# Two layers of a recommendation tower, turned from one tile of samples with samples on the partitions to two tiles with features on the partitions

## The chip, the cores and the metric

The kernel runs on one core of one Trainium2 chip. The metric is device time in microseconds. Short names: PE is TensorE, ACT ScalarE, DVE VectorE, POOL GpSimd, SP SyncE.

## What is computed

512 samples, each with 26 indices into 26 embedding tables of width 128 and one dense vector of width 128. Everything is f32.

```python
e = jnp.stack([tbl_0[ids[:, 0]], ..., tbl_25[ids[:, 25]]], axis=1)
combined = jnp.concatenate([dense_features[:, None, :], sparse_features], axis=1)
interactions = jnp.einsum('bfd,bgd->bfg', combined, combined)
z = interactions[:, iu, ju]                      # 351 pairs
h = jnp.concatenate([z, r_dense_features], axis=1)
h = jnp.maximum(h @ W_top1 + b_top1, 0.0)        # 479 -> 512
h = jnp.maximum(h @ W_top2 + b_top2, 0.0)        # 512 -> 256
y = h @ W_top3                                   # 256 -> 1
```

## The kernel before, in words

The samples form four tiles of 128 (`T = 4`). A factor of a product that must keep f32 accuracy is split in a rounded part "hi" and a rest "lo" (both f32r), and three products are taken: hi·hi, hi·lo, lo·hi. ACT makes the hi (a copy that rounds), DVE the lo (a subtraction).

**Selection.** For the 12 smallest tables (1000 rows) the lookup is a product of the table with one-hot rows: six steps of two tables, each 8 chunks of 125 rows, both parts, 512 samples as columns (`select_first`, `select_step`). The ids are spread over the partitions by a product (`spread_ids`) or by a DMA; DVE makes 7 of the 8 one-hot chunks of a step (`make_onehots`), ACT the eighth (`make_last_onehot`). Step 0 is written out in `select_first`: eight products of table 0's hi as the chunks come, with the ids of step 1 spread between the fourth and the fifth, then 24 more. `stage` holds 4 tables, `tab_hi` and `tab_lo` 4.

**Gathered rows.** The other 14 tables are gathered by POOL, 128 rows per indirect DMA, 14 per tile, 56 in all, in the order of the tiles into two row buffers. PE transposes them in groups of 4, 4, 4, 2 (`transpose_group(t, q)`), ACT and DVE copy the result to `feats` (`copy_turn`).

**Pairs.** `gram(t, h)` makes the pair products of a quarter of a tile, 32 products of 27 columns, in one of `GB = 3` PSUM banks; it waits for the pick three quarters back (`picked_by_dve`). ACT and DVE pick from it (`copy_picked`); DVE reorders a tile (`order_by_sample`), PE transposes it (`move_picked`), ACT and DVE split it (`split_hi`, `split_lo`).

**Layers.** Per tile: layer 1 is 15 products of 512 columns (3 for the dense vector, 12 for the pairs), samples on the output's partitions. Relu on ACT (`relu1`), four transposes on PE (`transpose_hidden`), the split, layer 2 as 12 products of 256 columns plus one that adds the bias (L465), and layer 3 as a multiply and row sum on DVE (`finish`). The last tile does layer 1 in two halves of 256 columns (L498 to L505). At the end y, a column per tile, is transposed on PE (L575), copied (L921) and stored.

Each engine works in the order in which its block is written. `turns` lists the users of the PSUM banks for transposes in their order. All waits are on semaphores; a later instruction of an engine never passes an earlier one.

## Time and profile before

| | |
|---|---|
| median of 3 runs | 113.29 us (112.92 to 114.68) |
| profiled execution | 114.23 us; its span 112.4 us |
| PE busy | 102.7 us (91%), weight loads beside it 79.6 us |
| DVE, ACT, POOL busy | 66.8, 56.9, 61.0 us |
| selection on PE ends | 58.2 us into the span |
| last gather of rows issued | 79.05 us |
| DMA moved | 13.12 MB, 117 GB/s over the span |

The span runs from the first to the last instruction of the profiled execution; 1.8 us of its time lie around it. The busy share of PE says that it nearly always has something in flight, not that it goes at its best pace: a product of 512 columns takes one duration at the higher clock and nearly twice that at the lower.

### The profile page before, as it was taken

To read this page: it belongs to the slowest core of one execution; us is meant where nothing else is said; L and a number is where in the kernel's file an instruction comes from. 1 tells how busy PE (TensorE), PEld (TensorE's weight loads), DVE (VectorE), ACT (ScalarE), POOL (GpSimd) and SP (SyncE) were. 2 spreads that over 40 slices of the span, in tenths; PEclk is the share of its full clock that TensorE was granted. 3 is DMA by queue.
4 is the path that set the end of the run, shared out by engine and by line. 5 is a ranking of instruction groups with operands and counts; after the bars stand their busy time and mean duration, and the time that the engine had idled before them with its cause. 6 is when DMAs were issued, how large, how long until landed. Compare 5 with 4: busy or idle time off the path is not lost.

```text
span 112.4 us, 3333 instructions
## 1 busy us (share of the span) xinstructions
PE 102.7 (91%) x1447; PEld 79.6 (71%) x1447; DVE 66.8 (59%) x113; ACT 56.9 (51%) x83; POOL 61.0 (54%) x63
## 2 busy tenths in 40 slices
PE   4679999999999999999999839999999999988981
PEld 4235777788888888888887627786868786668860
DVE  1499846999999998996001976326331652252132
ACT  2596900894984956998028427047014701152210
POOL 2787877777777777778777767777300000000000
PEclk9999999999999999999999985999999999999997
DMA  2999789999999995482121212222100000000000
GB/s 60 289 272 228 204 148 274 235 258 223 250 172 244 246 346 198 121 271 62 47 67 50 53 47 53 53 71 51 47 6 6 0 6 0 6 6 0 0 0 1
DMA packets 5885, 13.12 MB, mean 117 GB/s; under 512 B 1784, under 2 KB 2698, under 8 KB 5871
## 3 DMA queue, kind: packets, MB, share of 16 engines
q1 hardware_dynamic: 3018, 8.37, 27.1%
q0 software_dynamic: 1792, 3.67, 12.7%
q10 hardware_dynamic: 1060, 0.87, 5.4%
q8 instruction: 11, 0.18, 0.7%
q14 instruction: 4, 0.02, 0.1%
HBM read 12.89 MB, written 0.01 MB: 115 GB/s over the span
## 4 chain that ended last, share of the span: by engine, by line
PE 90%; DVE 4%; ACT 2%; issue 2%; POOL 0%; DVEq 0%; POOLq 0%
PE banks L369 33%; PE banks L407 11%; PE banks L352 6%; PE banks L389 6%; PE banks L344 4%; PE banks L438 4%; PE banks L444 3%; PE banks L439 3%; PE banks L329 3%; PE banks L470 3%; PE banks L415 2%; PE banks L317 2%; PE banks L471 2%; PE banks L477 1%; DVE ids_bc L825 1%
## 5 line engine op out<-in xcount | busy, mean ns | idle before, releaser
L308 POOL DMA_INDIRECT rows<-in_tbl,ids_sb x56 | 60.3, 1076 | 18.2 <-issue 16.1
L369 PE MATMUL banks<-onehots,tab_hi 125*128 125x512 f32 x80 | 31.6, 395 | 0.0
L369 PE MATMUL banks<-onehots,tab_lo 125*128 125x512 f32 x80 | 31.2, 390 | 0.0
L611 ACT ACTIVATE tab_hi<-stage 125x1024 fp32r<-125x1024 f32 (+1 forms) x12 | 11.9, 1016 | 11.6 <-PE banks L369 5.8
L369 PEld LDWEIGHTS banks<-onehots,tab_hi 125*128 125x128 f32 x80 | 15.0, 188 | 3.3 <-issue 0.4
L369 PEld LDWEIGHTS banks<-onehots,tab_lo 125*128 125x128 f32 x80 | 15.0, 188 | 3.0
L798 DVE TENSOR_SCALAR onehots<-ids_bc,row_of 125x1024 fp32r<-125x1024 f32 x21 | 14.3, 750 | 2.5 <-PE banks L352 2.4
L407 PEld LDWEIGHTS banks<-feats 128*27 128x27 f32 x1024 | 10.9, 106 | 6.3 <-DVE picked L815 3.3
L785 DVE TENSOR_TENSOR tab_lo<-stage,tab_hi 125x1024 fp32r<-125x1024 f32 x12 | 14.2, 1219 | 1.0 <-ACT tab_hi L611 1.0
L815 DVE COPY_PREDICATED picked<-second_of,banks 128x112 f32<-128x112 int32 x16 | 4.5, 281 | 16.8 <-ACT picked L668 16.8
L798 DVE TENSOR_SCALAR onehots<-ids_bc_h,row_of 125x1024 fp32r<-125x1024 int16 x21 | 14.4, 752 | 0.0
L407 PE MATMUL banks<-feats 128*27 128x27 f32 x1024 | 13.1, 194 | 0.8 <-issue 0.5
L668 ACT ACTIVATE picked<-banks 128x112 f32<-128x112 f32 x16 | 4.2, 263 | 18.5 <-PE banks L407 18.3
L644 ACT ACTIVATE feats<-banks 128x1024 f32<-128x1024 f32 x6 | 6.7, 1115 | 5.1 <-PE banks L369 5.1
L389 PE MATMUL banks<-ident,rows 128*128 128x128 f32 x56 | 8.6, 278 | 0.1
L779 DVE TENSOR_TENSOR onehots<-stage,onehots 128x1024 fp32r<-128x1024 f32 (+1 forms) x3 | 3.1, 1029 | 9.0 <-ACT onehots L605 9.0
L389 PEld LDWEIGHTS banks<-ident,rows 128*128 128x128 f32 x56 | 6.3, 141 | 1.8 <-issue 1.0
L661 ACT ACTIVATE feats<-banks 128x512 f32<-128x512 f32 (+1 forms) x10 | 6.5, 693 | 0.6 <-PE banks L389 0.6
L636 ACT ACTIVATE onehots<-distance 125x1024 fp32r<-125x1024 f32 x6 | 6.3, 1050 | 0.2 <-PE banks L369 0.2
L344 PE MATMUL banks<-onehots,tab_hi 125*128 125x512 f32 x8 | 4.8, 728 | 1.8 <-DVE onehots L798 1.8
L842 DVE TENSOR_TENSOR tab_lo<-banks,tab_hi 128x512 fp32r<-128x512 f32 (+1 forms) x5 | 2.9, 578 | 5.7 <-ACT tab_hi L653 5.7
L438 PE MATMUL banks<-onehots,pairs_hi 128*128 128x512 f32 x12 | 5.9, 491 | 0.0
(81 smaller groups left out, 131.6 us busy)
## 6 DMA issues: line engine op xcount, KB each, us to landing
stage<-in_tbl SPq DMA_DIRECT2D x11, 448.0 KB
stage<-in_w SPq DMA_DIRECT2D x3, 512.0 KB
rows<-in_tbl,ids_sb POOLq DMA_INDIRECT x56, 6.0
ids_bc_h<-ids_short_rows ACTq DMA_DIRECT2D x6, 128.0 KB, 6.6
stage<-in_tbl SPq DMA_DIRECT2D x11, 52.0 KB
stage<-in_tbl SPq DMA_DIRECT2D x2, 224.0 KB
dense_sb<-in_dense SPq DMA_DIRECT2D x1, 256.0 KB, 11.7
stage<-in_w SPq DMA_DIRECT2D x1, 256.0 KB
```

Source lines behind the costliest of these rows:

```text
L308: nc.gpsimd.indirect_dma_start(out=rows[:, t % RB, m, :], out_offset=None, in_=tables[m], in_offset=bass.IndirectOffsetOnAxis(ap=ids_sb[:, ...
L344: nc.tensor.matmul(bank(0, 0), tab_part(0, 0)[:, c, :], onehots[0:RP, c, 0, :], start=(c == 0), stop=False)
L352: last = nc.tensor.matmul(bank(0, k), tab_part(k, part)[:, c, :], onehots[0:RP, c, k, :], start=(part == 0 and c == 0), stop=(part == 1 an ...
L369: last = nc.tensor.matmul(bank(n, k), tab_part(i, part)[:, c, :], onehots[0:RP, c, k, :], start=(c == 0 and part == 0), stop=(c == CHUNKS ...
L389: last = nc.tensor.transpose(tr_ps(n)[:, c, :], rows[:, t % RB, m, :], ident[:])
L407: last = nc.tensor.matmul(gram_ps(u)[SLOT * s:SLOT * s + F, i, 0:F], x, x, start=True, stop=True)
L438: nc.tensor.matmul(l1_ps, x, w1_hi[:, k, :], start=False, stop=False)
L611: nc.scalar.activation(tab_part(i, 0)[:, first:, :], src[:, first:, :], ACT.Copy).then_inc(hi_ready, 1)
L644: nc.scalar.activation(dst, src, ACT.Copy).then_inc(selected_copied, 1)
L661: nc.scalar.activation(dst, src, ACT.Copy).then_inc(turn_by_act, 1)
L785: nc.vector.tensor_tensor(tab_part(i, 1), src, tab_part(i, 0).bitcast(f32), ALU.subtract).then_inc(lo_ready, 1)
L798: nc.vector.tensor_scalar(onehot(n, c), ids_of(n)[0:RP], row_of[:, c:c + 1], None, ALU.is_equal).then_inc(onehot_by_dve, 1)
```

## The change

Layers 1 and 2 now run for two tiles at once (`PT = 2`), with the features on the output's partitions: the weights are the stationary operand, and 256 samples are the columns. Layer 1 of a pair is four blocks `m` of 128 features, each 15 products of 256 columns; relu and split go straight from PSUM to the layer 2 operand, without the transposes. Layer 2 is 4 pieces of 6 products (two output blocks `m`), its bias is added by ACT and DVE with the relu (`relu2`), and layer 3 is two f32 products with a stationary operand of one column; y comes out as a row and is stored in two DMAs. `b_top2` and `W_top3` are loaded as four rows and turned once on PE (`turn_small`). The layers of tiles 0 and 1 start when both are split. Layer 2 of that pair stands ahead of the transposes of tile 3's last group. In the selection, WARM goes from 8 to 6 transposes of the identity, another six stand behind the first `spread_ids`, and two (`FILL`) behind each of the first seven products.

```diff
-    C1 = H1 // P
-    HH, CH = H1 // 2, C1 // 2
+    C1, C2 = H1 // P, H2 // P
+    PT = 2
+    PN = PT * P
+    NP = T // PT
...
-    WARM = 8
+    WARM = 6
+    FILL = 2
...
+    turns = [(t, q) for t in (0, 1) for q in range(NG)] + [moved(0), (2, 0), (2, 1), moved(1)]
+    turns += [(2, 2), (2, 3), (3, 0), (3, 1), moved(2), (3, 2), (3, 3), moved(3)]
...
+        def l1_ps(n):
+            return banks[:, 6 + n % 2, 0:PN]
+        def l2_ps(m):
+            return banks[:, 1 + m, 0:PN]
+        def y_ps(p):
+            return banks[0:1, 0, PN * p:PN * (p + 1)]
...
+                    if c < CHUNKS - 1:
+                        warm_up(FILL)
...
+            def turn_small():
+                pe.wait_ge(small_loaded, 32)
+                pe.wait_ge(ids_copied, BY_DMA)
+                nc.tensor.transpose(banks[:, 7, 0:2 * C2], b2w3_rows[:], ident[0:2 * C2, 0:2 * C2]).then_inc(
+                    rows_turned, 1)
...
+            def layer1_dense(p, m):
+                n = C1 * p + m
+                if n == 0:
                     pe.wait_ge(ids_copied, BY_DMA)
                     pe.wait_ge(dense_lo_ready, 1)
                     pe.wait_ge(lo_ready, S + 1)
+                elif n == 1:
+                    pe.wait_ge(b2w3_ready, 1)
...
+            def layer1(p, m):
+                n = C1 * p + m
+                cols = slice(P * m, P * (m + 1))
+                pe.wait_ge(pairs_hi_ready, PT * (p + 1))
+                for k in range(1, NK + 1):
+                    if n == 0:
                         pe.wait_ge(lo_ready, S + k // WS + 1)
+                    x = pairs_hi[:, k - 1, :, :]
+                    nc.tensor.matmul(l1_ps(n), w1_hi[:, k, cols], x, start=False, stop=False)
+                    nc.tensor.matmul(l1_ps(n), w1_lo[:, k, cols], x, start=False, stop=False)
+                pe.wait_ge(turn_by_dve, dve_turns(turns.index(moved(PT * p + 1)) + 1))
                 for k in range(1, NK + 1):
+                    last = nc.tensor.matmul(l1_ps(n), w1_hi[:, k, cols], pairs_lo[:, k - 1, :, :], start=False,
                                             stop=(k == NK))
                 last.then_inc(layer1_done, 1)
+            def layer2(p, c):
+                if c == 0 and p == 0:
                     pe.wait_ge(lo_ready, S + WV + 1)
+                if c == 0:
+                    pe.wait_ge(picked_by_dve, U * (T - 1) if p == 0 else U * T - 1)
+                pe.wait_ge(h1T_hi_ready, C1 * p + c + 1)
+                hi, lo = h1T_hi[p][:, c, :], h1T_lo[p][:, c, :]
+                for m in range(C2):
+                    cols = slice(P * m, P * (m + 1))
+                    nc.tensor.matmul(l2_ps(m), w2_hi[:, c, cols], hi, start=(c == 0), stop=False)
+                    nc.tensor.matmul(l2_ps(m), w2_lo[:, c, cols], hi, start=False, stop=False)
+                pe.wait_ge(h1T_lo_ready, C1 * p + c + 1)
+                for m in range(C2):
+                    cols = slice(P * m, P * (m + 1))
+                    last = nc.tensor.matmul(l2_ps(m), w2_hi[:, c, cols], lo, start=False, stop=(c == C1 - 1))
+                    if c == C1 - 1:
+                        last.then_inc(layer2_done, 1)
+            def layer3(p):
+                if p == 0:
+                    pe.wait_ge(picked_by_dve, U * T)
                 else:
+                    pe.wait_ge(y_ready, p)
+                for c in range(C2):
+                    pe.wait_ge(h2T_by_act if c == 0 else h2T_by_dve, p + 1)
+                    last = nc.tensor.matmul(y_ps(p), b2w3[:, C2 + c:C2 + c + 1], h2T[p][:, c, :], start=(c == 0),
+                                            stop=(c == C2 - 1))
+                last.then_inc(layer3_done, 1)
...
             spread_ids(0)
+            warm_up(WARM)
...
             gram(0, 2)
-            layer1_dense(0)
             gram(0, 3)
+            gram(1, 0)
             move_picked(0)
...
+            gram(1, 1)
+            gram(1, 2)
+            gram(1, 3)
+            transpose_group(2, 0)
+            transpose_group(2, 1)
+            turn_small()
+            layer1_dense(0, 0)
+            move_picked(1)
+            transpose_group(2, 2)
+            transpose_group(2, 3)
+            layer1(0, 0)
+            layer1_dense(0, 1)
+            layer1(0, 1)
+            gram(2, 0)
+            layer1_dense(0, 2)
+            layer1(0, 2)
+            gram(2, 1)
+            gram(2, 2)
+            gram(2, 3)
+            transpose_group(3, 0)
+            transpose_group(3, 1)
+            layer1_dense(0, 3)
+            layer1(0, 3)
+            move_picked(2)
+            transpose_group(3, 2)
+            for c in range(C1):
+                layer2(0, c)
+            transpose_group(3, 3)
+            for h in range(U):
+                gram(3, h)
+            layer1_dense(1, 0)
+            layer1_dense(1, 1)
+            move_picked(3)
+            layer1(1, 0)
+            layer3(0)
+            layer1(1, 1)
+            layer2(1, 0)
+            layer1_dense(1, 2)
+            layer1(1, 2)
+            layer2(1, 1)
+            layer1_dense(1, 3)
+            layer1(1, 3)
+            layer2(1, 2)
+            layer2(1, 3)
+            layer3(1)
...
+            def hidden_hi(p, m):
+                n = C1 * p + m
+                act.wait_ge(layer1_done, n + 1)
+                nc.scalar.activation(h1T_hi[p][:, m, :], l1_ps(n), ACT.Relu).then_inc(h1T_hi_ready, 1)
+            def relu2(p):
+                act.wait_ge(layer2_done, C2 * p + 1)
+                nc.scalar.activation(h2T[p][:, 0, :], l2_ps(0), ACT.Relu, bias=b2w3[:, 0:1]).then_inc(h2T_by_act, 1)
...
             make_hi(S + 2)
+            copy_picked(1, 0)
             split_hi(0)
             for v in range(3, WV + 1):
                 make_hi(S + v)
...
+            copy_picked(1, 1)
+            copy_picked(1, 2)
+            copy_picked(1, 3)
+            copy_turn(2, 0)
+            copy_turn(2, 1)
+            copy_small()
+            split_hi(1)
+            hidden_hi(0, 0)
+            hidden_hi(0, 1)
+            copy_picked(2, 0)
+            hidden_hi(0, 2)
+            copy_picked(2, 1)
+            copy_picked(2, 2)
+            copy_picked(2, 3)
+            copy_turn(3, 0)
+            copy_turn(3, 1)
+            hidden_hi(0, 3)
+            split_hi(2)
+            relu2(0)
+            for h in range(U):
+                copy_picked(3, h)
+            split_hi(3)
+            for m in range(C1):
+                hidden_hi(1, m)
+            relu2(1)
...
+            def hidden_lo(p, m):
+                n = C1 * p + m
+                dve.wait_ge(h1T_hi_ready, n + 1)
+                nc.vector.scalar_tensor_tensor(h1T_lo[p][:, m, :], l1_ps(n), 0.0, h1T_hi[p][:, m, :].bitcast(f32),
+                                               ALU.max, ALU.subtract).then_inc(h1T_lo_ready, 1)
+            def relu2(p):
+                if p == 0:
+                    dve.wait_ge(b2w3_ready, 1)
+                dve.wait_ge(layer2_done, C2 * p + 2)
+                nc.vector.tensor_scalar(h2T[p][:, 1, :], l2_ps(1), b2w3[:, 1:2], 0.0, ALU.add, ALU.max).then_inc(
+                    h2T_by_dve, 1)
...
             split_lo(0)
             for v in range(3, WV + 1):
                 make_lo(S + v)
...
+            for h in range(U):
+                copy_picked(1, h)
+            order_by_sample(1)
+            split_lo(1)
+            copy_turn(2, 2)
+            copy_turn(2, 3)
+            hidden_lo(0, 0)
+            hidden_lo(0, 1)
+            copy_picked(2, 0)
+            hidden_lo(0, 2)
+            copy_picked(2, 1)
+            copy_picked(2, 2)
+            copy_picked(2, 3)
+            order_by_sample(2)
+            hidden_lo(0, 3)
+            split_lo(2)
+            copy_turn(3, 2)
+            relu2(0)
+            copy_turn(3, 3)
+            for h in range(U):
+                copy_picked(3, h)
+            order_by_sample(3)
+            split_lo(3)
+            hidden_lo(1, 0)
+            copy_y(0)
+            for m in range(1, C1):
+                hidden_lo(1, m)
+            relu2(1)
+            copy_y(1)
```

Three places show how the instructions now stand. **The start on PE**, before the second step of the selection; `ident` is the identity (the transposes of `warm_up`), `pairs_hi` holds the ids here. Before:

```order
L317 MATMUL banks<-ident 128x128 x8
L329 MATMUL banks<-pairs_hi,ident_r 128x512 x2
L344 MATMUL banks<-onehots,tab_hi 128x512 x4
L329 MATMUL banks<-pairs_hi,ident_r 128x512 x2
L344 MATMUL banks<-onehots,tab_hi 128x512 x4
L352 MATMUL banks<-onehots,tab_hi 128x512 x8
L352 MATMUL banks<-onehots,tab_lo 128x512 x16
L329 MATMUL banks<-pairs_hi,ident_r 128x512 x2
```

And with the change, up to the id-spread for step 1:

```order
L318 MATMUL banks<-ident 128x128 x6
L330 MATMUL banks<-pairs_hi,ident_r 128x512 x2
L318 MATMUL banks<-ident 128x128 x6
L345 MATMUL banks<-onehots,tab_hi 128x512
L318 MATMUL banks<-ident 128x128 x2
L345 MATMUL banks<-onehots,tab_hi 128x512
L318 MATMUL banks<-ident 128x128 x2
L345 MATMUL banks<-onehots,tab_hi 128x512
L318 MATMUL banks<-ident 128x128 x2
L345 MATMUL banks<-onehots,tab_hi 128x512
L318 MATMUL banks<-ident 128x128 x2
L330 MATMUL banks<-pairs_hi,ident_r 128x512 x2
```

The products of chunks 0 to 6 now have two transposes of the identity behind each, and six more stand between the first id-spread and the first product.

**DVE after tile 0's pairs** (`stage3`, `w2` and `w` hold the second layer's weights, `picked1` the pairs of tile 1). Before:

```order
L825 STREAM_TRANSPOSE ids_bc0<-picked0 128x512
L779 TENSOR_TENSOR onehots<-stage2,onehots 128x512
L832 TENSOR_TENSOR pairs_lo0<-banks,pairs_hi0 128x512
L772 TENSOR_TENSOR w2_lo<-stage3,w2_hi 128x1024
L898 SCALAR_TENSOR_TENSOR b2_rows<-b2_hi,minus_lower,b2_sb 2x256
L815 COPY_PREDICATED picked1<-second_of,banks 128x14x8 x4
```

And with the change:

```order
L805 STREAM_TRANSPOSE ids_bc0<-picked0 128x512
L759 TENSOR_TENSOR onehots<-stage2,onehots 128x512
L812 TENSOR_TENSOR pairs_lo<-banks,pairs_hi 128x4x128
L752 TENSOR_TENSOR w2_lo<-stage3,w2_hi 128x1024
L795 COPY_PREDICATED picked1<-second_of,banks 128x14x8 x4
L805 STREAM_TRANSPOSE ids_bc1<-picked1 128x512
```

The order is the same but for the bias row (L898), which is gone; what moves is PE's order beside it.

**PE between tile 0's last transposes of rows and tile 1's pairs** (`feats` are pair products, 32 to a quarter, each of them two instructions in the trace; the transposes with `ids_bc` are `move_picked`). Before:

```order
L419 MATMUL banks<-onehots,dense_hi 128x512
L420 MATMUL banks<-onehots,dense_hi 128x512
L421 MATMUL banks<-onehots,dense_lo 128x512
L407 MATMUL banks<-feats 27x27 x32
L415 MATMUL banks<-ident,ids_bc 128x128 x4
L407 MATMUL banks<-feats 27x27 x32
L438 MATMUL banks<-onehots,pairs_hi 128x512
L439 MATMUL banks<-onehots,pairs_hi 128x512
L438 MATMUL banks<-onehots,pairs_hi 128x512
L439 MATMUL banks<-onehots,pairs_hi 128x512
L407 MATMUL banks<-feats 27x27 x32
```

And with the change:

```order
L414 MATMUL banks<-feats 27x27 x96
L422 MATMUL banks<-ident,ids_bc 128x128 x4
L414 MATMUL banks<-feats 27x27 x96
L392 MATMUL banks<-ident,rows 128x128 x8
L429 MATMUL banks<-ident,b2w_rows 128x4
L445 MATMUL banks<-dense_hi,onehots 128x256
L446 MATMUL banks<-dense_lo,onehots 128x256
L447 MATMUL banks<-dense_hi,onehots 128x256
L422 MATMUL banks<-ident,ids_bc 128x128 x4
```

Layer 1's products of tile 0 stood between the quarters of tile 1; now a quarter of tile 1 stands ahead of `move_picked(0)` and the other three follow it back to back, ahead of every product of layer 1.

## Rows read from the trace of the kernel before

**Rows 1.** the page: the chain that ended last, by engine.
```profile
PE 90%; DVE 4%; ACT 2%; issue 2%; POOL 0%; DVEq 0%; POOLq 0%
```

**Rows 2.** timeline to 22 us: start, length, engine, line, count, idle before.
```profile
1.52 1.97 PE L317 MATMUL banks<-ident 128*128 128x128 f32 x8 [1.52 <-POOL ident L299]
...
2.54 0.42 DVE L861 CAST pairs_hi<-feats 12x512 fp32r<-12x512 int32 x1 [0.66 <-DMA feats<-in_ids_rows]
...
3.42 1.22 PE L329 MATMUL banks<-pairs_hi,ident_r 12*128 12x512 f32 x2
...
5.51 4.74 DVE L798 TENSOR_SCALAR onehots<-ids_bc,row_of 125x1024 fp32r<-125x1024 f32 x7
...
6.41 2.69 PE L344 MATMUL banks<-onehots,tab_hi 125*128 125x512 f32 x4 [1.77 <-DVE onehots L798]
...
12.05 3.61 PE L352 MATMUL banks<-onehots,tab_hi 125*128 125x512 f32 x8
...
15.46 3.90 PE L352 MATMUL banks<-onehots,tab_lo 125*128 125x512 f32 x16
...
19.94 0.50 PE L369 MATMUL banks<-onehots,tab_hi 125*128 125x512 f32 x1
...
21.05 1.06 ACT L611 ACTIVATE tab_hi<-stage 125x1024 fp32r<-125x1024 f32 x1 [0.54 <-DMA stage<-in_tbl]
```

**Rows 3.** ACT's timeline, the second step's share (same columns).
```profile
23.87 1.12 ACT L644 ACTIVATE feats<-banks 128x1024 f32<-128x1024 f32 x1
```

**Rows 4.** chain of waits, in the selection: start, length, what.
```profile
27.51 0.44 PE banks L389 x4
...
58.21 1.06 ACT feats L644
```

**Rows 5.** windows of PE: us, busy (instructions), granted clock, DMA share, GB/s.
```profile
67.00:68.00 1.00, 1.00 (x43) 0.50 0.22 57
...
70.00:71.00 1.00, 1.00 (x57) 0.87 0.28 66
```

**Rows 6.** PE's timeline round the pause after tile 0.
```profile
66.64 0.96 PE L415 MATMUL banks<-ident,ids_bc 128*128 128x128 f32 x4 [1.80 <-DVE ids_bc L825]
```

**Rows 7.** DVE's timeline in the same place.
```profile
69.21 1.23 DVE L772 TENSOR_TENSOR w_lo<-stage,w_hi 128x1024 fp32r<-128x1024 f32 x1 [0.25 <-ACT w_hi L599]
...
70.75 0.27 DVE L815 COPY_PREDICATED picked<-second_of,banks 128x112 f32<-128x112 int32 x1
```

**Rows 8.** ACT's timeline in the same place.
```profile
68.13 1.05 ACT L599 ACTIVATE w_hi<-stage 128x1024 fp32r<-128x1024 f32 x1
```

**Rows 9.** PE's timeline: a tile at full clock, the last tile, the end.
```profile
85.99 0.74 PE L407 MATMUL banks<-feats 128*27 128x27 f32 x64
86.66 1.09 PE L389 MATMUL banks<-ident,rows 128*128 128x128 f32 x8
...
90.33 0.38 PE L465 MATMUL banks<-b_rows,ones 2*128 2x256 f32 x1
90.65 0.39 PE L470 MATMUL banks<-w_hi,tab_hi 128*128 128x256 f32 x1
...
101.61 0.39 PE L498 MATMUL banks<-onehots,pairs_hi 128*128 128x256 f32 x1 [0.69 <-ACT pairs_hi L674]
101.83 0.28 PE L499 MATMUL banks<-onehots,pairs_hi 128*128 128x256 f32 x1
101.95 0.28 PE L498 MATMUL banks<-onehots,pairs_hi 128*128 128x256 f32 x1
...
110.00 0.38 PE L575 MATMUL banks<-ident,y 128*4 128x128 f32 x2 [0.59 <-DVE stage L852]
```

**Rows 10.** weight loads by line: count, busy, mean ns, idle before.
```profile
L498 PEld LDWEIGHTS banks<-onehots,pairs_hi 128*128 128x128 f32 x8 | 1.5, 188 | 0.9 <-ACT pairs_hi L674 0.9
```

**Rows 11.** DVE's last row, same columns.
```profile
110.42 0.37 DVE L921 COPY stage<-banks 4x128 f32<-4x128 f32 x1 [0.47 <-PE banks L575]
```

**Rows 12.** POOL's last gather of rows.
```profile
79.05 0.94 POOL L308 DMA_INDIRECT rows<-in_tbl,ids_sb  x1 [0.30 <-issue]
```

## What the change should do to the time

> **What bounds the kernel now.** I read the page's chain of waits first: 90% of it lies on PE and 4% on DVE [rows 1]. So it is PE's own work and pauses that count, and the other engines only where PE waits for them. Then the timeline of the first 22 us, to see which clock PE works at; the chain in the selection; PE, DVE and ACT round PE's one long pause; and PE in an undisturbed tile and at the end. Three things are to be seen.
>
> First, the start runs at PE's lower clock. Eight products of 512 columns lie between 12.05 and 15.46, 0.43 us each, which is 1.2 GHz; from 15.46 sixteen take 3.90, 0.235 each, which is 2.4 GHz [rows 2]. The second step's first product starts at 19.94. Before about 10 us the products stand 0.66 apart ([rows 2]: four in 2.69) because DVE makes a one-hot every 0.68 (seven in 4.74).
>
> Second, the selection then runs without a gap to 58.2, and the rest to the end of DVE's last instruction, 110.42 + 0.37 = 110.79, takes 52.6 [rows 4, 11].
>
> Third, within this rest PE pauses 1.80 us before 66.64 [rows 6]; the clock is at 0.50 (1.2 GHz) at 67 and is back at 2.4 GHz within the slice at 70 [rows 5]. An undisturbed quarter of pair products takes 86.66 - 85.99 = 0.67, a product of 256 columns 0.115, a transpose 0.44/4 = 0.11, and where PE turns to another kind of work the first step is 0.1 longer (101.61 to 101.83 against 101.95) [rows 4, 9].
>
> **The sum, against the profiled execution (114.23 us).**
>
> *1. Id-spread earlier: -0.4.* The ids are ready at 2.54 + 0.42 = 2.96, but the spread waits for eight transposes until 3.42 [rows 2]. With six it starts at about 3.0, and DVE's one-hots at 5.1.
>
> *2. Transposes between the first products: -1.3 with step 1 in it.* The six further transposes (about 0.21 each at the lower clock) fill PE's wait. A chunk with its two is 0.43 + 2 x 0.21 = 0.85 at the lower clock, 0.46 at the higher; DVE delivers every 0.68. So PE has no gap from about 6.0, where it now has none only from the second id-spread on. The question is when the clock rises. Before, it rose at about 15.5, some 5 us after the gaps ended; after the pause it rose about 4 us after 66.64 [rows 2, 5, 6]. From 6.0 that gives 10 to 11, perhaps 7 if the work ahead of 5.4 counts. With a rise at 11, chunk 4 is under way; three more chunks take 0.46 each and 24 products 0.235 each, and with the id-spread (0.65) the second step starts near 18.6, 1.3 earlier; with a rise at 7 it starts near 16.9, 3.1 earlier; with none before 15.5 at 20.7, 0.75 later, since the added transposes then cost and give nothing. I take a gain of 1.7, near the later rise, which has the better row.
>
> There is a cap. ACT's rounding of table 5 waits for its DMA until 21.05, and three ACT instructions later the copy of step 0 ends at 23.87 + 1.12 = 24.99 [rows 2, 3], which step 2 waits for. With four transposes (0.44) step 2 can start at 25.4 instead of 27.95 [rows 4]. So at most 2.5 of the 3.1 survive. DVE needs 7 x 0.68 + 2 x 1.2 = 7.2 a step against PE's 7.7, so the gain is kept to the end of the selection. Terms 1 and 2: **-1.7**, ends -2.5 and +0.75.
>
> *3. The tail, in the times of the trace (its start left at 58.2).* Up to tile 0's third quarter nothing changes. The fourth quarter and tile 1's first then go before the pause, which stays for the same cause (DVE's reorder of tile 0, before 66.64 [rows 6]); I put `move_picked(0)` at 66.25. Two quarters follow, until 68.15. Then tile 1's fourth quarter needs DVE's pick of its first (three banks). On DVE that pick stands behind the split of `w2`, which starts at 69.21 and takes 1.23, behind ACT's rounding (68.13 + 1.05) [rows 7, 8]. Before, the pick ran at 70.75 and hurt nobody, since layer 1's products stood between. Now PE waits from 68.15 to about 69.95: a **new pause of 1.8 us**. The quarter ends at 70.65, where before it ended at about 75.0 with tile 0's 12 layer products done.
>
> From there, all at the higher clock: 40 transposes x 0.115 = 4.6; layer 1, 8 blocks x 15 x 0.115 = 13.8; layer 2, 48 x 0.117 = 5.6; layer 3, two f32 products of 256 columns twice. The f32 product of 128 columns at 110.00 takes 0.38 with its pipeline's end, 0.21 without [rows 9], so 4 x 0.43 = 1.7; ends 1.5 and 2.2. Eight quarters x 0.67 = 5.4; about 20 changes of kind x 0.1 = 2.0. Pauses: the copy of tile 3's last group on DVE before its pairs 0.6; reorder before `move_picked(3)` 0.7; the split after it 0.7 (the row at 101.61 has that same wait [rows 9]); relu before layer 3 0.6. Then the copy of y, 0.5. Sum 36.2, end at 106.9, against 110.79: -3.9.
>
> What this tail leaves out is in there: sixteen hidden transposes (1.8), four bias products (90.33 to 90.65, 0.32 each, 1.3 [rows 9]) and the y transposes with their wait (1.0), less layer 3 (1.7).
>
> *4. The clock in the tail: +1.4.* The old pause cost one stretch at 1.2 GHz, and that is in 110.79. The new one comes 1.9 us later and should keep the clock down until 73 or 74. The work there is a quarter (0.94 instead of 0.67), eight transposes (+0.8) and a few layer products (+0.3). Ends: nothing, and 2.6 if two stretches fall outside the pauses. Terms 3 and 4: **-2.5**, ends -3.9 and -1.0.
>
> *What costs nothing.* The layer 2 block that stands ahead of tile 3's last transposes only keeps PE off POOL: the last gather is issued at 79.05 [rows 12], PE comes there near 88, so neither order waits. The turn of the small rows is one short transpose. Relu and split of 256 columns on ACT and DVE lie beside the next block's 15 products (1.7 us), and layer 1 alternates two banks. The first half of y is stored beside PE's work.
>
> Sum: 114.23 - 1.7 - 2.5 = 110.0. The profiled execution lies 0.94 above the median, so the median should be **109.1 us**.
>
> **A rule against this change.** The last tile already has layer 1 products of 256 columns: sixteen weight loads of 0.188 each [rows 10] lie in stretches where the products are 0.115 apart [rows 9], so loads overlap and splitting 512 into twice 256 is free. The Trainium skill (TensorE: Matmul & The Clock Gate, section Back-to-back issue gap) says that load and product set the spacing together, about 81 ns at 128 columns and 131 at 512. By that rule two of 256 cost well above one of 512, and an estimate from those figures makes layer 1 dearer by about half, the sum by 7 us. The trace's 0.115 is half of its 0.235, which speaks against it.
>
> **Rivals.**
> - *The clock does not rise earlier in the selection.* Terms 1 and 2 become 0 to +0.75. For: until 10 us PE worked with short gaps before too, and the clock did not rise. Time: 109.1 + 2.0 = 111.1. Chance 0.15.
> - *The tail gives back what it saves.* DVE's order makes tile 1 pay longer, the clock stays low twice, and waits for relu and split between layers add up. Tail -0.5, time 111.1. Chance 0.18. Both of these together: 113.2, chance 0.06.
> - *Both go better:* clock up near 7, none lost in the tail: 109.1 - 0.8 - 1.4 = 106.9. Chance 0.05.
> - *Slower: weight loads become the bound of the layers.* If a load could not start before its predecessor ended, each of the 120 layer 1 products would take 0.188 instead of 0.115 [rows 9, 10]: +8.7, time 117.8. It decides from a spacing of 0.115 + 4.2/120 = 0.15 on. For: the stationary operand is now a strided slice of `w1`, which no row shows, and every load is a new one. Against: the last tile. The rule above is a milder form of it. Chance 0.03.
> - The forecast itself, 107.9 to 110.4: chance 0.53.
>
> **How the numbers follow.** A measurement of this kernel tells 2% (2.3 us) from no change. Faster means under 111.0: the forecast, the better case, half of each of the two rivals at 111.1 and none of the rest: 0.53 + 0.05 + 0.16 = 0.74. Slower: the loads, and a part of what I have not seen: 0.04. Same: 0.22. The range from 107.4 to 112.2 leaves out the better case's lower part, the double miss and the loads.
>
> **What would show it.** Right: the 24 products of the first step start near 12.4 instead of 11.6 but at 0.235 each; the second step before 18.8; the selection ends near 56.5; a second PE pause of over 1.5 us before tile 1's fourth quarter, released by DVE's pick, with `w2`'s split ahead of it; clock 0.50 for more than one stretch round it; layer products 0.115 to 0.12 apart; no wait for gathered rows in tile 3; from the selection's end to DVE's last copy about 50.1. Wrong: products of 256 columns over 0.15 apart, a clock that rises only at 15, or layer blocks that wait for relu and split.

## The result, and the profile after

The changed kernel is **slower**: 116.94 us median of five runs (116.6 to 120.5) against 114.13 us of the kernel before in the same runs; the ratio is 1.031, 95% interval 1.022 to 1.040. (Executions of either kernel fall in a shorter and a longer group; the ratio compares the means of the shorter ones, 116.9 and 113.4, here and in every ratio below.) Forecast were 109.1 us and a range up to 112.2. The profiled execution took 119.35 us, span 117.5, so it lies 2.4 above the median; the executions at 116.6 to 116.9 have spans of 114.7 to 115.0. A later profile of the same kernel, below, has a start that is 2.6 us shorter.

The page: PE's row, the granted clock in 40 slices, the instruction queue, the chain by engine (it answers [rows 1]).

```profile
PE 104.1 (89%) x1497; PEld 86.4 (74%) x1497; DVE 67.4 (57%) x109; ACT 55.8 (47%) x82; POOL 61.9 (53%) x63
...
PEclk9999999999999999999999687559999999599999
...
q8 instruction: 12, 0.20, 0.7%
...
PE 81%; issue 7%; ACT 5%; DVE 4%; POOL 0%; DVEq 0%; POOLq 0%
```

"issue" is 7% of the chain, 8 us, where it was 2%. The clock is low in three stretches of the tail (in windows: 65 to 69, 72 to 79 and 99 to 103 us), where it was in one. PE works 1.4 us longer in all, so most of the loss is standing still. PE's timeline at the start (columns: start, length, engine, line, count, idle before it), for [rows 2]:

```profile
3.00 1.21 PE L330 MATMUL banks<-pairs_hi,ident_r 12*128 12x512 f32 x2
...
8.42 0.63 PE L318 MATMUL banks<-ident 128*128 128x128 f32 x2
...
14.12 1.99 PE L355 MATMUL banks<-onehots,tab_hi 125*128 125x512 f32 x8
15.95 3.79 PE L355 MATMUL banks<-onehots,tab_lo 125*128 125x512 f32 x16
19.67 0.72 PE L330 MATMUL banks<-pairs_hi,ident_r 12*128 12x512 f32 x2
```

The first id-spread is at 3.00, as forecast, but a product with its two transposes stays at 0.85 us until 14.12, and the second step starts at 20.32, 0.4 later than before, not 1.7 earlier. The row at 19.67 is the third id-spread, the last work ahead of the second step. The column of the granted clock reads 1.00 in windows from 7 to 17 us all the same, so I read the clock of the start from the spacing: 512 columns take 0.43 at the lower clock and 0.23 at the higher. Then PE's tail, from the last product of the selection to the end:

```profile
58.20 0.39 PE L372 MATMUL banks<-onehots,tab_lo 125*128 125x512 f32 x1
...
62.24 1.46 PE L414 MATMUL banks<-feats 128*27 128x27 f32 x90
65.00 1.71 PE L414 MATMUL banks<-feats 128*27 128x27 f32 x102 [1.30 <-issue]
67.26 1.12 PE L422 MATMUL banks<-ident,ids_bc 128*128 128x128 f32 x4 [0.55 <-DVE ids_bc L805]
68.31 2.06 PE L414 MATMUL banks<-feats 128*27 128x27 f32 x128
71.46 0.35 PE L414 MATMUL banks<-feats 128*27 128x27 f32 x21 [1.09 <-DVE picked L795]
72.50 0.76 PE L414 MATMUL banks<-feats 128*27 128x27 f32 x43 [0.69 <-issue]
73.19 1.97 PE L392 MATMUL banks<-ident,rows 128*128 128x128 f32 x8
...
75.67 0.41 PE L446 MATMUL banks<-dense_lo,onehots 128*128 128x256 f32 x1
75.88 0.41 PE L447 MATMUL banks<-dense_hi,onehots 128*128 128x256 f32 x1
```

```profile
85.54 1.15 PE L414 MATMUL banks<-feats 128*27 128x27 f32 x112 [0.21 <-issue]
...
89.46 0.28 PE L457 MATMUL banks<-pairs_hi,onehots 128*128 128x256 f32 x1 [0.91 <-issue]
...
95.21 2.06 PE L414 MATMUL banks<-feats 128*27 128x27 f32 x211 [0.81 <-issue]
99.28 0.70 PE L414 MATMUL banks<-feats 128*27 128x27 f32 x45 [2.02 <-issue]
...
103.27 0.39 PE L457 MATMUL banks<-pairs_hi,onehots 128*128 128x256 f32 x1 [0.69 <-ACT pairs_hi L665]
...
114.38 1.02 PE L491 MATMUL banks<-distance,b2w 128*1 128x256 f32 x4 [0.54 <-ACT distance L644]
```

A quarter of pair products is x64. The new pause that I forecast before tile 1's fourth quarter is there, released by DVE's pick, with 1.09 us. But there are five more that nothing releases: 1.30 after 90 rows of L414, 0.69 after 21, 0.21 after 80, 0.91 in the middle of a layer 1 block, and 2.02 after 211 rows that had no pause among them. Together 5.13 us. None is at the edge of a quarter, where PE's program has its waits. (The 0.81 before 95.21 is called "issue" too, but stands at such an edge, where PE waits for DVE's copy of tile 3's last group; I had forecast 0.6 for it.) Layer products of 256 columns are 0.12 apart at the higher clock, and there is no wait for gathered rows. DVE's last instruction:

```profile
115.44 0.59 DVE L830 COPY y_row<-banks 1x256 f32<-1x256 f32 x1 [1.08 <-PE banks L491]
```

It ends at 116.03. From the selection's end at 58.6 that is 57.4 us; before it was 52.6 ([rows 4, 11]), and forecast was 50.1.

### The profile page after: what moved, and what is told of

It is laid out like the page before. It is cut to its first block, busy times and chain, and to the rows that moved or that the text cites. A ratio compares the mean times of both kernels' runs of the same rounds, so it can differ in the third digit from the quotient of the medians.

```text
span 117.5 us, 3417 instructions
## 1 busy us (share of the span) xinstructions
PE 104.1 (89%) x1497; PEld 86.4 (74%) x1497; DVE 67.4 (57%) x109; ACT 55.8 (47%) x82; POOL 61.9 (53%) x63
## 4 chain that ended last, share of the span: by engine, by line
PE 81%; issue 7%; ACT 5%; DVE 4%; POOL 0%; DVEq 0%; POOLq 0%
PE banks L372 31%; PE banks L414 7%; PE banks L392 5%; PE banks L355 5%; PE banks L457 4%; PE banks L318 4%; PE banks L345 3%; PE banks L458 3%; PE banks L461 3%; PE banks L422 3%; PE banks L330 3%; PE banks L445 2%; PE banks L491 2%; PE banks L475 2%; PE banks L476 2%
## 5 line engine op out<-in xcount | busy, mean ns | idle before, releaser
L309 POOL DMA_INDIRECT rows<-in_tbl,ids_sb x56 | 61.1, 1090 | 18.1 <-issue 16.2
L372 PE MATMUL banks<-onehots,tab_hi 125*128 125x512 f32 x80 | 31.7, 396 | 0.0
L414 PE MATMUL banks<-feats 128*27 128x27 f32 x1024 | 13.3, 198 | 6.6 <-issue 5.0
L414 PEld LDWEIGHTS banks<-feats 128*27 128x27 f32 x1024 | 11.4, 110 | 9.1 <-issue 6.5
L818 DVE SCALAR_TENSOR_TENSOR tab_lo<-banks,tab_hi 128x256 fp32r<-128x256 f32 x8 | 3.4, 425 | 14.0 <-ACT tab_hi L640 14.0
L640 ACT ACTIVATE tab_hi<-banks 128x256 fp32r<-128x256 f32 x8 | 3.1, 384 | 15.5 <-PE banks L461 15.5
L457 PE MATMUL banks<-pairs_hi,onehots 128*128 128x256 f32 x32 | 8.6, 299 | 1.6 <-issue 0.9
L392 PE MATMUL banks<-ident,rows 128*128 128x128 f32 x56 | 9.8, 313 | 0.0
L318 PE MATMUL banks<-ident 128*128 128x128 f32 x26 | 7.5, 424 | 1.5 <-POOL ident L300 1.5
L392 PEld LDWEIGHTS banks<-ident,rows 128*128 128x128 f32 x56 | 7.8, 162 | 0.8
L458 PE MATMUL banks<-pairs_hi,onehots 128*128 128x256 f32 x32 | 8.1, 284 | 0.0
```

The costliest lines, as they stand in the source:

```text
L309: nc.gpsimd.indirect_dma_start(out=rows[:, t % RB, m, :], out_offset=None, in_=tables[m], in_offset=bass.IndirectOffsetOnAxis(ap=ids_sb[:, ...
L318: nc.tensor.transpose(banks[:, 4, 0:P], ident[:], ident[:])
L372: last = nc.tensor.matmul(bank(n, k), tab_part(i, part)[:, c, :], onehots[0:RP, c, k, :], start=(c == 0 and part == 0), stop=(c == CHUNKS ...
L392: last = nc.tensor.transpose(tr_ps(n)[:, c, :], rows[:, t % RB, m, :], ident[:])
L414: last = nc.tensor.matmul(gram_ps(u)[SLOT * s:SLOT * s + F, i, 0:F], x, x, start=True, stop=True)
L457: nc.tensor.matmul(l1_ps(n), w1_hi[:, k, cols], x, start=False, stop=False)
```

## Theories

**Theory A: delivery of instructions.** A row of PE is a weight load and a product, so two instructions; a quarter is 128 in 0.67 us, a layer block of 15 products 30 in 1.75. The instruction queue (q8) moved 12 packets, 0.20 MB, that is 16 KB each; I take one for a block of 256 instructions. If one block is fetched while the one before it runs, and takes longer than two quarters, PE stands still wherever the 256th instruction falls. From row 90 of 62.24 to row 21 of 71.46 there are 102 + 4 + 128 + 21 = 255 rows, 510 instructions: two blocks but for two, and the program's own waits, which are instructions too, stand in no row. The kernel before has a quarter between each two blocks of layer 1; the changed one has four in a row, twice. **Rivals:** the pauses are waits for banks, picks or copies; the clock; the new start; layers of two tiles cost more by themselves.

The Trainium skill (Runtime: NRT & Kernel Launch, section Instruction fetch mechanics) describes refills of 16 KiB, 256 instructions, and calls the cost of crossing a block "mostly hidden". The block's size fits these traces; whether it is hidden is what the experiments ask.

The trace has the packets themselves. Behind the last gather of rows nothing else of this size moves, so that 16 GB/s in a window of 1 us is one packet (windows: us, busy (instructions) of PE, PEld, DVE, ACT, POOL, then clock, DMA share, GB/s):

```profile
96.00:97.00 1.00, 1.00 (x137) 1.00 (x124) 0.41 (x2) 0.52 (x2) 0.00 (x0) 1.00 0.07 16
...
98.00:99.00 1.00, 0.00 (x0) 0.00 (x0) 0.00 (x0) 0.00 (x0) 0.00 (x0) 1.00 0.00 0
```

Packet by packet, each of the five pauses ends 2.4 to 2.8 us after a packet of 16 KB on q8 begins and 1.3 to 1.5 after it has landed; the 0.81 before 95.21 has no packet near it (4.4 us). Counted from PE's first row, the five stand behind rows 470, 725, 976, 1,103 and 1,356: 255, 251, 127 and 253 rows apart, one or two blocks each time.

**How to read the experiments.** When they ran, the kernel before took 137 to 141 us (medians), and the changed one 138.5. The profiles of that time show where it is lost (PE's timeline of the kernel before, run again):

```profile
65.62 0.78 PE L407 MATMUL banks<-feats 128*27 128x27 f32 x46 [0.98 <-ACT feats L644]
...
71.85 0.33 PE L407 MATMUL banks<-feats 128*27 128x27 f32 x5 [1.10 <-issue]
```

Between about 60 and 86 us (in some runs up to 92) pair products come in groups of five or so rows with pauses of 0.4 and 1.1 us, in every kernel, and PE is at 0.50 of its clock for most of it; ACT and DVE wait too, and some runs have such pauses in the selection from 34 us on. Behind it all is as in the first profiles. So I compare ratios to the kernel before from runs made beside it, and in traces the start (to 20 us) and the tail: from the first reorder transposes (line L415 or L422, four of them) to the span's end.

## The experiments

**Both kernels again.**

> The changed kernel itself once more, beside the runs of the kernel before in the same call, since both take 20% longer in these calls than when they were first timed. If what made it 3% slower (bunches of pair products that outrun the delivery of PE's instructions, in theory A) weighs the same here, the ratio is again 1.02 to 1.04. If the long disturbed stretch that all kernels of these calls show between about 42 and 80 us takes in the same instructions, the ratio is within 1% of 1. In its profile the pauses behind the disturbed stretch (middle of tile 2's last quarter, of layer 1, and 2.0 us in tile 3's second quarter) stay at the products where they were.

> The kernel before once more, for its profile in this state: by theory A its pauses with nothing as releaser lie only in the disturbed stretch, and behind it (from tile 1's layer 1 on) there is none over 0.5 us, as in its first profile.

Ratio 1.014 (1.004 to 1.024), between what the two readings expected. The tails: before 135.0 - 88.96 = 46.0 us; changed 136.2 - 87.89 = 48.3, with one quarter already done. In the changed kernel's tail (PE's timeline) the pauses stand behind the same rows as in its first profile:

```profile
108.34 0.28 PE L457 MATMUL banks<-pairs_hi,onehots 128*128 128x256 f32 x1 [0.92 <-issue]
...
114.09 2.06 PE L414 MATMUL banks<-feats 128*27 128x27 f32 x211 [0.81 <-issue]
118.44 0.57 PE L414 MATMUL banks<-feats 128*27 128x27 f32 x45 [2.29 <-issue]
```

In the kernel before the only such pause behind the disturbed stretch is 0.49 us, behind row 1,228. The start came out another way than in the first profile:

```profile
7.53 0.63 PE L318 MATMUL banks<-ident 128*128 128x128 f32 x2
...
8.38 0.40 PE L318 MATMUL banks<-ident 128*128 128x128 f32 x2
...
11.52 2.00 PE L355 MATMUL banks<-onehots,tab_hi 125*128 125x512 f32 x8
13.37 3.79 PE L355 MATMUL banks<-onehots,tab_lo 125*128 125x512 f32 x16
17.08 0.72 PE L330 MATMUL banks<-pairs_hi,ident_r 12*128 12x512 f32 x2
```

The clock rises at 8.4 us, and the third id-spread is at 17.08 instead of 19.67: 2.6 us, about what the shorter executions of the first result lie below its profile.

**The pace by itself.** Behind the last product:

```
+ for h in range(8):
+     ...  # one quarter of pair products, into a bank nobody reads
```

> The changed kernel with eight more quarters of pair products (8 x 128 = 1,024 PE instructions, eight times the 0.67 us of a quarter = 5.4 us of work) behind its last product, where PE waits for nobody and nobody for PE; their result is not used. It measures the disputed cost by itself. Theory A (blocks of 256 instructions, 3.4 to 3.9 us from block to block): PE works for two quarters (1.3 us), stands still for some 2.2 us with nothing as its releaser, and so on: the added stretch takes 12 to 15 us, with pauses 256 instructions (128 products' records, x128) apart. Rival (pair products have no limit but their own time, and the pauses were waits for banks, picks or copies): the added stretch takes 5.4 us and has no pause.

PE's timeline, and windows of all engines (columns as above):

```profile
135.78 2.18 PE L567 MATMUL banks<-feats 128*27 128x27 f32 x235
140.64 1.42 PE L567 MATMUL banks<-feats 128*27 128x27 f32 x128 [2.67 <-issue]
144.37 1.71 PE L567 MATMUL banks<-feats 128*27 128x27 f32 x128 [2.31 <-issue]
148.37 0.40 PE L567 MATMUL banks<-feats 128*27 128x27 f32 x15 [2.29 <-issue]
```

```profile
137.50:138.50 1.00, 0.47 (x57) 0.36 (x43) 0.00 (x0) 0.00 (x0) 0.00 (x0) 1.00 0.05 16
138.50:139.50 1.00, 0.00 (x0) 0.00 (x0) 0.00 (x0) 0.00 (x0) 0.00 (x0) 1.00 0.00 0
139.50:140.50 1.00, 0.00 (x0) 0.00 (x0) 0.00 (x0) 0.00 (x0) 0.00 (x0) 1.00 0.00 0
140.50:141.50 1.00, 0.86 (x99) 0.86 (x103) 0.00 (x0) 0.00 (x0) 0.00 (x0) 0.95 0.00 0
141.50:142.50 1.00, 0.56 (x47) 0.43 (x37) 0.00 (x0) 0.00 (x0) 0.00 (x0) 0.50 0.07 16
```

128 rows, 256 instructions, then a pause of 2.3 us, twice, with no wait in the program: 3.7 and 4.0 us from block to block. (The first stretch holds nearly two blocks before its pause of 2.67.) Round each point at which PE runs dry 16 KB are moved (16 GB/s over 1 us), and PE goes on 2.4 to 2.9 us after that packet begins. The eight quarters take 13.4 us (135.36 to 148.77) instead of 5.4. The rival falls. The Trainium skill's "mostly hidden" does not hold for such a run of products, whatever it is elsewhere: the measurement decides.

**Quarters in a row, in the kernel before.**

```
+ layer1_hi(t - 1, range(1, 3)); layer1_hi(t - 1, range(3, NK + 1)); layer1_lo(t - 1)
+ gram(t, 0); gram(t, 1); gram(t, 2); gram(t, 3)
```

> The kernel before with one thing moved: the four quarters of pair products of tiles 1 to 3 stand in one row, behind the tile's layer 1 products, where each quarter before stood between two blocks of layer 1. No work is added or left out. Theory A (delivery of instructions): 512 PE instructions now want to pass in 2.7 us; in each of the three tiles a pause of about 2 us with nothing as its releaser appears in the middle of a quarter, and the clock falls after some of them: the total grows by 3 to 5 us. Rival 1 (the pauses of the changed kernel come from its pairs of tiles, not from the bunches): no such pause, the total within 1 us of the kernel before, or up to 1.5 us longer since the fourth quarter waits for DVE's pick of the first (three banks), with DVE as its releaser.

Ratio 1.052 (1.045 to 1.059), tail 143.4 - 92.86 = 50.5 us, 4.5 longer than before's. PE's timeline:

```profile
103.13 0.54 PE L407 MATMUL banks<-feats 128*27 128x27 f32 x42 [1.90 <-issue]
...
116.03 1.02 PE L407 MATMUL banks<-feats 128*27 128x27 f32 x96 [2.47 <-issue]
...
129.41 0.36 PE L407 MATMUL banks<-feats 128*27 128x27 f32 x21 [1.88 <-issue]
```

One pause of about 2 us in each tile's bunch, inside a quarter, 6.25 in all, behind rows 723, 975 and 1,356. Neither pairs of tiles nor the new start are in this kernel. This shows the bunch as the cause of such pauses. Two things came out otherwise than expected: the clock stayed at 1.00 behind all three, and the total grew by 7 us, not 3 to 5. I put only the tail's 4.5 to the bunches: tile 0's first quarter, up to which both programs are the same, starts at 68.81 against 65.62 in the kernel before, so the ratio overstates them.

**Other work in the pause.**

```
  for h in range(U):
+     if h == 2: ...  # eight products of 512 columns into bank 4
      gram(3, h)
```

> The changed kernel with eight more products of 512 columns (8 x 0.235 = 1.88 us at the higher clock, 16 PE instructions) between the second and the third quarter of tile 3's pair products, into a bank that nobody reads then; their result is not used. Theory A (delivery of instructions): PE stood still 2.0 us in that bunch for its next block of instructions; the added work runs in the time in which the block is on its way, so the total changes by no more than 0.3 us, or falls a little if the clock stays up, and what is left of the pause is under 0.5 us. Rival (the pause is a wait for a bank, a pick or a copy on another engine, which the added work doesn't touch either, or PE's own work counts in full): if PE counts in full the total grows by 1.9 us.

PE's timeline:

```profile
116.42 1.32 PE L414 MATMUL banks<-feats 128*27 128x27 f32 x128 [0.81 <-issue]
117.66 2.12 PE L549 MATMUL banks<-onehots,dense_hi 128*128 128x512 f32 x8
119.72 1.40 PE L414 MATMUL banks<-feats 128*27 128x27 f32 x128
```

The 2.3 us pause is gone, and the 128 rows behind the added work run through. From tile 3's first quarter (116.42) to the span's end it takes 21.8 us; the changed kernel, from 114.09, takes 22.1. Ratio 0.993 (0.989 to 0.997), where the changed kernel has 1.014, though from runs made at another time. The tail is 138.2 - 91.98 = 46.2 us, 2.1 shorter than the changed kernel's with 2.1 us more work in it. The pause pays for the added work; the rest is the clock: in windows it is 0.50 for the first 2 us of this tail, and in the changed kernel's repeated profile for 2.4 us and again, from 93.7, for 3.4. That second stretch lies ahead of the added work, so its absence here is not the work's doing. If the pause had been a wait for another engine's data, the work could have hidden in it too; with the pace measured above, and the shift below, that reading is left without support.

**The old start.**

```
- WARM = 6; FILL = 2
+ WARM = 8
```

> The changed kernel with the start of the kernel before: eight transposes in one block, none between the first products, none ahead of the second id-spread. Everything from the second step on is the changed kernel's. Theory A (the stream of PE's instructions is delivered in blocks of 16 KB, 256 instructions, and a bunch of pair products, 128 instructions in 0.67 us, outruns it): the pauses released by nothing ('issue') inside the bunches stay, but each moves later in the program by nine f32 products (36 instructions, since 18 transposes are missing ahead of them): in tile 1's bunch the pauses after product 10 or 11 of a quarter come after about product 19 or 20, and the 2.0 us pause of tile 3's second quarter (after product 10) comes after about product 19. The time: the second step starts 0.4 us earlier (19.9 against 20.3), and the total is 0.4 to 1.5 us shorter. Rival 1 (the pauses are waits for banks or picks): they stay at the same product of the same quarter. Rival 2 (the new start makes the later clock worse, and the tail follows from it): the pauses go and the total falls by 3 us or more. By my prediction's term 1 and 2 the total would be 1.7 us longer.

PE's timeline:

```profile
113.56 2.23 PE L411 MATMUL banks<-feats 128*27 128x27 f32 x229 [0.81 <-issue]
117.40 0.40 PE L411 MATMUL banks<-feats 128*27 128x27 f32 x27 [1.61 <-issue]
```

229 rows instead of 211: 18 more, and 18 transposes are missing some 100 us earlier. The stop is behind row 1,356 of the program, as in the changed kernel, and I see nothing but a count of instructions that ties the two. Of the changed kernel's stops, 3.7 us in all (0.17, 0.27, 0.92 and 2.29), this one of 1.61 is left, and the tail is 135.0 - 88.88 = 46.1 us against 48.3, with the same work in it and a clock that is low for longer (to 96.7): so where the blocks end can be worth about 2 us. Its four executions (136.8 to 145.4 us) lie too far apart for a ratio. In tile 1's bunch, where I expected a pause behind another row, there is none: a miss. Third id-spread at 18.92.

**w2's split behind the picks.**

> The changed kernel with one piece of order moved: the split of w2 (ACT's rounding, DVE's difference) stands behind tile 1's picks instead of ahead of the second of them, so that DVE's pick of tile 1's first quarter no longer waits for it. By my prediction's term 3 the pause of 1.1 us before tile 1's fourth quarter (released by DVE's pick) goes and the total falls by 1.1 to 1.8 us. Theory A (delivery of instructions): the quarter then starts earlier but runs into the end of its block sooner; the pause with nothing as its releaser after about product 21 of that quarter grows from 0.7 to about 1.8 us, and the total stays within 0.4 us of the changed kernel's.

PE's timeline:

```profile
92.29 1.92 PE L414 MATMUL banks<-feats 128*27 128x27 f32 x149
95.43 0.56 PE L414 MATMUL banks<-feats 128*27 128x27 f32 x43 [1.23 <-issue]
```

The wait for DVE is gone; PE runs 149 = 128 + 21 rows, to the same instruction as before, and waits 1.23 us there, where the changed kernel had 1.52 for the pick and 0.17 there. So the wait moved to the block's end, as theory A says, but it is shorter (expected: 1.8). The tail is 139.4 - 91.24 = 48.2 against 48.3, with a stretch of low clock near its end that the other lacks; the ratio, 0.997 (0.986 to 1.007), leans the other way. What that order is worth stays open between nothing and 1.7%.

**The new start alone, in the kernel before**, timed twice:

> The kernel before with the changed kernel's start alone: six transposes, two between the first products of the first step, six ahead of the second id-spread. My prediction's terms 1 and 2: 1.7 us shorter. What the changed kernel's trace says: the second step starts at 20.3 instead of 19.9, the total 0.3 to 0.5 us longer. If the block boundaries of PE's instructions (18 transposes are 36 instructions more) matter in the tail, the pause at 64.47 inside tile 0's fourth quarter moves by nine products and may fall at another place with another length: up to 1 us either way.

> The kernel before with the changed kernel's start alone, once more in five rounds. The profiles say that the clock rises at 8.4 to 9.5 us with the new start (five profiles of six) and at 14.2 to 16.2 us with the old one, and that the second step starts 1.6 us earlier; what ends the disturbed stretch may take that back. If the gain reaches the end: ratio 0.985 to 0.99. If the disturbed stretch (60 to 85 us) swallows it: 1.00, as in three rounds (1.003).

Third id-spread at 17.01 and 17.92 us, against 18.70 in the kernel before, yet the ratios are 1.003 (0.991 to 1.016) and 1.004 (0.999 to 1.009). It seems that the disturbed stretch takes it back: in the two repeated kernels the first quarter of tile 0 starts at 65.62 and 65.78, though PE had ended the selection 5.6 us apart. In the second it is there that PE waits:

```profile
65.78 0.78 PE L414 MATMUL banks<-feats 128*27 128x27 f32 x46 [5.08 <-ACT feats L631]
```

So the start is read from the traces, and that its gain reaches the end no run shows: over all profiles the third id-spread is at 18.70 to 19.53 (four with the old start) and at 17.01 to 18.10 (nine with the new one), except 19.67 in the one that came with the result.

**Quarters put apart.** Two versions of the changed kernel. The second one's order:

```
+ layer1_dense(0, 2); transpose_group(3, 0); gram(2, 2); transpose_group(3, 1); layer1(0, 2)
+ layer1_dense(0, 3); gram(2, 3); transpose_group(3, 2); transpose_group(3, 3)
+ layer2_part(0, (0, 1)); gram(3, 0); layer1(0, 3); move_picked(2); gram(3, 1)
+ layer2_part(0, (2, 3)); layer2_part(1, (0, 1)); gram(3, 2); layer2_part(1, (2,))
+ gram(3, 3); layer2_part(1, (3,)); layer1_dense(1, 0); layer1_dense(1, 1); move_picked(3)
```

> The changed kernel (pairs of tiles in the layers, its start, all its products) with the quarters of pair products of tiles 1 to 3 put apart: a quarter stands between the six transposes of the next tile, between layer 1 and layer 2 of the first pair, between the parts of layer 2, and so on, so that no more than one or two quarters stand in a row. The layer 2 sums of the first pair share one bank, and the copy of tile 1's picks stands ahead of the split of w2. Theory A (PE's instructions are delivered in blocks of 256 and bunches outrun it): the pauses released by nothing inside tile 1's and tile 3's quarters (1.3, 0.7, 0.9 and 2.0 us in the changed kernel's profile) fall under 0.5 us each, and the total is 1.5 to 4 us shorter than the changed kernel's, within 1.5 us of the kernel before. Rival (the pauses come from banks, picks or the copy, or the layers in pairs cost more by themselves): the total stays within 1 us of the changed kernel's, 3% over the kernel before.

> The changed kernel with the quarters of tiles 1 to 3 put apart more evenly than in the version with one or two quarters in a row: tile 3's transposes stand ahead of layer 1's last block of the first pair, and each of tile 3's quarters has six or more layer products in front of it. Theory A: behind the disturbed stretch the pauses with nothing as releaser (1.0, 1.3 and 0.6 us in the first spread version, 2.3 and 0.9 in the changed kernel) add up to under 1 us; the total is 1 to 2 us below the first spread version's, 0.5 to 1.5% below the kernel before. Rival: the pauses stay, since they hang on banks and picks, whose order has hardly changed; the total is that of the first spread version (ratio 1.00 to 1.01).

> The evenly spread version of the changed kernel once more, in five rounds, since the runs so far gave no interval for it (135.9 us twice, against 139.4 to 140.9 of the kernel before). If the spread pays for the whole change (no bunch, layers in pairs kept, new start kept), the ratio to the kernel before is 0.97 to 0.99. If those two runs were luck, it is 1.00 to 1.01, as for the first spread version.

The first: 1.006 (0.997 to 1.014), pauses 1.04, 1.34 and 0.56 behind the disturbed stretch, more than the 0.5 expected; the first of them stands at a quarter's edge, the others behind rows 1,229 and 1,357. The second, timed again: 0.988 (0.983 to 0.994). In its first profile the tail is 134.1 - 89.12 = 45.0; in the profile of the second timing it is 46.6, with one more stretch of lower clock (119.6 to 123.3). All pauses of the first profile's tail with nothing as releaser, PE's timeline:

```profile
108.50 0.73 PE L413 MATMUL banks<-feats 128*27 128x27 f32 x64 [0.78 <-issue]
...
112.15 0.40 PE L413 MATMUL banks<-feats 128*27 128x27 f32 x26 [0.42 <-issue]
```

Of these 1.2 us (expected: under 1) the 0.78 stands ahead of tile 3's first quarter, where PE waits for the copy of tile 3's last group, as at 0.81 in the changed kernel. Inside quarters 0.42 is left, where the changed kernel's repeated profile has 3.7 in all. The same operations in another order: from 1.4% slower to 1.2% faster than the kernel before, the latter less than the 2% that I call a difference. It has not been timed beside the changed kernel, nor where the kernel before takes 114 us.

**What is common to them.** All fourteen profiles have such a stop behind the disturbed stretch or, in the first two, in the tail: 0.15 us or more, nothing as releaser, no wait of the program at its place. In all of them it stands behind the same rows of PE's program, whatever work is there: 469 or 470, 722 to 725, 975 or 976, 1,103, 1,228 or 1,229, 1,356 or 1,357 (and, in the run with eight added quarters, 1,738, 1,866 and 1,994). Each ends 2.2 to 2.9 us after a packet of 16 KB on q8 begins. No bank, pick or copy is common to these places.

## Why the prediction was wrong

- **Terms 1 and 2 (start, -1.7): right as far as the third id-spread, though not in the first profile.** The clock rose at 8.3 to 10.5 us in the nine other profiles with the new start, mostly earlier than my 10 to 11, and the third id-spread came 1.7 us earlier on average (17.4 against 19.1). In the profile that came with the result it rose at 14.1, the rival's case; the 2.6 us by which the other executions are shorter fit the early rise, but they have no trace, so that is argued, and the new start alone gained nothing that could be measured. What the clock looks for I can't say: the same program had both.
- **Term 3 (tail, -3.9): the step that failed.** I took each quarter at 0.67 us wherever it stands, and a row of [rows 9] bore that out, but there the quarter stood alone. In a row they are bound by the delivery of instructions, 3.7 to 4 us for two. That put in 5.13 us of pauses which the sum did not have (the first, 1.30, fell for the most part into the wait for DVE's reorder of tile 0, which the sum had). The hint was in the trace: 2% of "issue" in [rows 1], one such pause (0.29) in tile 0's four quarters, the only bunch that the kernel before had; there is another of 0.20 in a lone quarter of tile 3.
- The pauses that the sum did have came near: the pick 1.09 (1.52 run again) for 1.8, the copy 0.81 for 0.6, the split 0.69 for 0.7, relu 0.54 for 0.6. The reorder before `move_picked(3)`, 0.7 in the sum, was hidden (0.60 run again). Near were also layer 3 (1.02 each, with its end) and the spacing of layer products.
- **Term 4 (clock, +1.4): mis-sized, as a consequence.** The clock fell three times, each time behind pauses. The tail missed by 7.3 us (57.4 for 50.1). Tile 1's fourth quarter starts 1.1 later than forecast (71.46, less the 0.4 by which the tail began later, for 69.95); the first pause and the lower clock from 65 to 69 are both in that. The other four pauses are 3.8. Most of the rest, some 2.4 us, I put down to the lower clock behind that point: eight transposes took 1.97 against 1.09 [rows 9], layer products 0.21 apart against 0.12. An estimate from such rows at both levels makes it 3.7 us for the stretches of 72.5 to 79 and 99.3 to 102.6, of which the term had allowed 1.4. That part is not measured by itself. (The term's range is off too: -3.9 + 2.6 is -1.3, not -1.0.)
- **Rivals.** "The tail gives back what it saves" had the sign (chance 0.18) but the wrong mechanism and size: its waits were DVE's. The weight loads did not become the bound: 0.12 apart, against the rule cited there. No rival had the delivery of instructions, and the 0.04 for slower named one mechanism only.

Sum: 109.1 with the tail's miss of 7.3 is 116.4, against 116.9 measured. The tail is that of the profiled execution, the start that of the others; that they go together is argued.

## What to carry to other kernels

Count instructions, not only time, where short products stand in a row: where 256 instructions of PE wanted to pass in less than about 3.5 us, it stopped, and where it stopped depended on the count from the program's beginning. (In the kernel before, two packets begin 3.5 us apart, near 82 and 85 us, and PE does not stop between them; where stop follows stop they lie 3.7 to 4.0 apart. Other engines were not tried.) Work that takes long per instruction (512 columns) between them hid 2.1 us of delivery for nothing; moving it away, as this change did, is what costs. A pause with nothing as its releaser in the middle of a loop is worth a look at its row number before any wait is tuned.

## What the runs showed of the hardware

- In a run of short products (27 columns) PE stopped after every 256 instructions once it had used what was there: stops 3.7 and 4.0 us apart, pauses 2.3 us, each ended 2.2 to 2.9 us after a 16 KB packet of the instruction queue began.
- Such stops stood behind the same row numbers of PE's program (725, 1,103 and 1,356, give or take two) in kernels with different work there.
- A pause can cost more than itself, but need not: behind the 2.02 us one at 99.28 the clock was 0.50 for over 3 us, behind the 2.29 us one of the same kernel at 118.44 it stayed at 2.4 GHz, and so it did behind 1.90, 2.47 and 1.88 us in the kernel with its quarters in a row.
- The same program's clock rose at 8.4 us in one execution and at 14.1 in another.
- In the later runs all kernels had a stretch of some 25 us in which instructions came in small groups. In each it ends in tile 0's last quarter or tile 1's first. Its cause is open, and so is how the ratios would come out without it, but for the changed kernel itself (1.031 there, 1.014 here).
